# Tiles 6 and 7 joined on VectorE, and the last dense bank split by expert, in a one-core attention and mixture-of-experts kernel

## The reference

```
h = layernorm(x) * (1 + ca) + sa
x = x + ga * attention(h)            # 16 query heads, 4 key/value groups, causal
h = layernorm(x) * (1 + cb) + sb
logits = h @ gate_w.T                # 8 experts, the best two, softmax over the two
out = x + gb * sum over the two of  w_f * (expert_w[e_f] @ h + expert_b[e_f])
```

## Time and profile before

| | |
|---|---|
| median of 3 runs | 882.91 us (882.91 to 884.2) |
| profiled execution, its own time | 882.36 us |
| its span | 880.2 us |
| busy: TensorE, VectorE, ScalarE, GpSimd | 98%, 84%, 62%, 37% of the span |
| chain that ended last, by engine | TensorE 91%, VectorE 4%, ScalarE 1%, GpSimd 1%, DMA 1% |

### The profile page before, as it was taken

One profiled execution on the slowest core, in us unless ns is written; L12 is line 12 of the kernel. 1 busy time (PEld: TensorE's weight loads), 2 busy tenths in 40 slices (PEclk: granted clock), 3 DMA queues, 4 the chain that ended last, 5 costly groups with the idle time before them and its releaser, 6 DMA issues.

```text
span 880.2 us, 17025 instructions
## 1 busy us (share of the span) xinstructions
PE 863.9 (98%) x5433; PEld 772.0 (88%) x5433; DVE 741.2 (84%) x1686; ACT 541.9 (62%) x1249; POOL 325.9 (37%) x398
## 2 busy tenths in 40 slices
PE   8999999999999999999999999999999999999996
PEld 7888888888888888888888998999988888889995
DVE  6878888888888888878878888988888989888777
ACT  5686666666666666664666666666666666665462
POOL 3744122222222222140534444444422222577565
PEclk9999999999999999999999999999999999999999
DMA  7000800000000000300000000000000000442494
GB/s 270 1 12 14 287 13 13 13 12 12 12 12 12 12 12 13 108 7 7 0 26 13 14 13 13 13 13 14 13 13 13 9 6 13 150 151 89 140 285 128
DMA packets 37201, 43.34 MB, mean 49 GB/s; under 512 B 3104, under 2 KB 34366, under 8 KB 37054
## 3 DMA queue, kind: packets, MB, share of 16 engines
q1 hardware_dynamic: 34776, 36.20, 12.9%
q0 software_dynamic: 2304, 6.29, 2.3%
q10 hardware_dynamic: 56, 0.02, 0.0%
HBM read 32.28 MB, written 15.20 MB: 54 GB/s over the span
## 4 chain that ended last, share of the span: by engine, by line
PE 91%; DVE 4%; ACT 1%; issue 1%; POOL 1%; DMA 1%; POOLq 0%; SPq 0%; ACTq 0%
PE ps_t L1092 14%; PE ps_s L976 8%; PE ps_s L980 8%; PE ps_s L977 8%; PE ps_o L968 7%; PE ps_o L972 7%; PE ps_o L969 7%; PE ps_m L976 4%; PE ps_m L980 4%; PE ps_m L977 4%; PE ps_m L968 3%; PE ps_m L972 3%; PE ps_m L969 3%; PE ps_o L1102 1%; PE ps_t L976 1%
## 5 line engine op out<-in xcount | busy, mean ns | idle before, releaser
L1447 ACT ACTIVATE pt_hi<-ps_t 128x512 fp32r<-128x512 f32 (+2 forms) x320 | 170.8, 534 | 124.7 <-PE ps_t L1092 124.2
L1497 ACT ACTIVATE probs<-ps_s,neg_max 128x128 f32<-128x128 f32 (+7 forms) x256 | 189.8, 742 | 79.6 <-DVE neg_max L1893 76.7
L1902 DVE TENSOR_TENSOR pt_lo<-ps_t,pt_hi 128x512 fp32r<-128x512 f32 (+2 forms) x320 | 192.1, 601 | 13.0 <-ACT pt_hi L1447 9.0
L1893 DVE TENSOR_REDUCE neg_max<-ps_s 128x1 f32<-128x128 f32 (+7 forms) x256 | 192.3, 751 | 3.7
L724 POOL TENSOR_TENSOR q_lo<-raw,q_hi 128x512 fp32r<-128x512 f32 x60 | 77.4, 1289 | 310.6 <-ACT q_hi L1447 310.6
L1092 PE MATMUL ps_t<-ident,probs 128*128 128x128 f32 x1152 | 188.6, 272 | 0.9 <-DVE pt_lo L1902 0.9
L1092 PEld LDWEIGHTS ps_t<-ident,probs 128*128 128x128 f32 x1152 | 141.8, 141 | 20.5 <-DVE pt_lo L1902 4.9
L976 PE MATMUL ps_s<-k_hi,q_hi 128*128 128x512 f32 (+2 forms) x354 | 148.5, 419 | 2.4 <-ACT probs L1497 2.4
L1940 DVE SCALAR_TENSOR_TENSOR acc<-ps_m,rsum,acc 128x256 f32<-128x256 f32 x256 | 111.3, 476 | 16.3 <-PE ps_m L980 15.7
L980 PE MATMUL ps_s<-k_hi,q_lo 128*128 128x512 f32 (+2 forms) x354 | 123.4, 349 | 0.0
L1887 DVE TENSOR_TENSOR ps_s<-ps_s,mask 128x128 f32<-128x128 f32 x256 | 75.4, 295 | 56.7 <-PE ps_s L980 49.2
(11 more groups left out here) (341 smaller groups left out, 1717.5 us busy)
## 6 DMA issues: line engine op xcount, KB each, us to landing
slot_out_dram<-y_slot SPq DMA_DIRECT2D x38, 128.0 KB, 1.8
wq_raw<-in_L_attn_wq_dram SPq DMA_DIRECT2D x32, 128.0 KB, 2.3
wo_raw<-in_L_attn_wo_dram SPq DMA_DIRECT2D x32, 128.0 KB, 2.0
wkv_raw<-in_L_attn_wkv_dram SPq DMA_DIRECT2D x2, 1024.0 KB, 6.4
acc<-in_L_attn_x_dram SPq DMA_DIRECT2D x2, 1024.0 KB, 16.7
we_raw<-in_L_ffn_expert_w_dram SPq DMA_DIRECT2D x1, 2048.0 KB, 8.6
slot_rows<-slot_rows_dram SPq DMA_DIRECT2D x2, 1024.0 KB, 8.4
slot_rows_dram<-in_L_attn_x_dram SPq DMA_DIRECT2D x1, 1920.0 KB, 15.9
```

Of the source, the lines that this page charges most:

```text
L1447: return nc.scalar.activation(dst, src, ACT.Copy, scale=scale)
L1497: nc.scalar.activation(probs[par][:, prob_offset(i):prob_offset(i) + w], ps_s[:, i % 2, col:col + w], ACT.Exp, bias=neg_max[:, par, i:i + ...
L1893: nc.vector.tensor_reduce(neg_max[:, par, i:i + 1], ps_s[:, i % 2, col:col + w], AXIS_X, ALU.max, negate=True).then_inc(max_set, 1)
L1902: nc.vector.tensor_tensor(pt_lo[:, q % PT, lo:CH], ps_t[:, q % 2, lo:CH], pt_hi[:, q % PT, lo:CH].bitcast(F32), ALU.subtract).then_inc(pt_ ...
```

## The change

- GpSimd joins no tile; `weigh(j)` and `join_part` treat all tiles alike. Tiles 6 and 7 are weighted once on ScalarE and joined on VectorE, behind the last slot and before experts 6 and 7 of dense tile 1. SyncE stores them before dense tile 1.
- VectorE's join 8 goes into tile 2's mix, behind expert 5; join 9 behind tile 2's finish; joins 10 and 11 behind the last tile. ScalarE weights tile 9 before `mix_first(3)`.
- The last bank of dense tile 3 (experts 6 and 7) is made in two groups of 256 columns: expert 6 in the late bank, expert 7 in `ps_o`. `finish_last` adds both rows after expert 5 into `y_even`, then expert 6 and expert 7 to that sum, then gb and the residual.

```diff
@@ constants
-POOL_JOINS = (6, 7)
+SLOT_JOINS = 6
@@ SyncE
-            in_slots = joins_by(SLOTS1) // JOIN_OPS
-            for j in range(joins_by(SLOTS1 - 1) // JOIN_OPS, in_slots):
+            for j in range(joins_by(SLOTS1 - 1) // JOIN_OPS, NT):
                 store_joined(j)
             store_mixed(1)
-            for j in range(in_slots, NT):
-                store_joined(j)
+            store_joined(NT)
             store_mixed(2)
-            for j in range(NT, JOINS - 1):
+            for j in range(NT + 1, JOINS - 1):
                 store_joined(j)
             store_mixed(3)
             store_joined(JOINS - 1)
@@ GpSimd (pool_join is removed)
-            for lo, hi in ((0, NT), (NT, JOINS)):
-                for j in range(lo, hi):
-                    gather(j)
-                for j in POOL_JOINS:
-                    if lo <= j < hi:
-                        pool_join(j)
+            for j in range(JOINS):
+                gather(j)
@@ TensorE, experts(d, e2)
-                bank = late_bank(d, e2)
-                pair = slice(2 * e2, 2 * e2 + 2)
...
+                last_pair = 2 * e2 + 2 == EXPERTS and d + 1 == HALF
+                for lo in range(2 * e2, 2 * e2 + 2, 1 if last_pair else 2):
+                    these = slice(lo, lo + 1 if last_pair else lo + 2)
+                    bank = late_bank(d, e2)[:, 0:(these.stop - lo) * O] if lo % 2 == 0 else ps_o[:, 0:O]
+                    if lo % 2:
+                        pe.wait_ge(slot_out, ALL_SLOTS)
...
+                    last.then_inc(moe_mm, 1)
@@ ScalarE
                 if s + 2 == ALL_SLOTS:
-                    weigh(POOL_JOINS[0], 0)
-                    weigh(POOL_JOINS[0], 1)
-            weigh(POOL_JOINS[1], 0)
+                    weigh(SLOT_JOINS)
+            weigh(SLOT_JOINS + 1)
             slot_finish(ALL_SLOTS - 1)
-            weigh(POOL_JOINS[1], 1)
             hidden2_hi(3)
             mix_first(2)
             weigh(NT)
+            weigh(NT + 1)
             mix_first(3)
-            for j in range(NT + 1, JOINS):
-                weigh(j)
+            weigh(NT + 2)
+            weigh(NT + 3)
@@ VectorE
+            def finish_last():
+
+                d, par = HALF - 1, (HALF - 1) % 2
+                y = y_even[:, par, :]
+                dve.wait_ge(mixed, d * LATER_MIXES + LATER_MIXES - 2)
+                nc.vector.tensor_tensor(y, y, y_odd[:, par, :], ALU.add).then_inc(mixed, 1)
+                for e, bank in ((EXPERTS - 2, late_bank(d, EXPERTS // 2 - 1)), (EXPERTS - 1, ps_o)):
+                    dve.wait_ge(moe_mm, d * 4 + 4 + e % 2)
+                    dve.wait_ge(mixed, d * LATER_MIXES + e - 1)
+                    nc.vector.scalar_tensor_tensor(y, bank[:, 0:O], coef[:, d, e:e + 1], y,
+                                                   ALU.mult, ALU.add).then_inc(mixed, 1)
+                dve.wait_ge(mixed, d * LATER_MIXES + LATER_MIXES + 1)
+                nc.vector.tensor_tensor(y_sum[:, d, :], y, row_of["gb1"], ALU.mult).then_inc(ysum_set, 1)
+                dve.wait_ge(ysum_set, 2 * d + 1)
+                nc.vector.tensor_tensor(y_sum[:, d, :], y_sum[:, d, :], acc[:, NT + HALF + d, :],
+                                        ALU.add).then_inc(yout_set, 1)
...
+            for j in range(SLOT_JOINS, NT):
+                join(j)
             mix(1, {}, range(2 * DENSE_EARLY, EXPERTS))
             finish(1)
             hidden2_lo(3)
-            mix(2, {})
+            mix(2, {5: (NT,)})
             finish(2)
-            join(NT)
-            mix(3, {3: (NT + 1,), 5: (NT + 2,)})
-            finish(3)
-            if JOINS - 1 not in POOL_JOINS:
-                join(JOINS - 1)
+            join(NT + 1)
+            mix(3, {}, range(2, EXPERTS - 2))
+            finish_last()
+            join(NT + 2)
+            join(JOINS - 1)
```

More of the change, by code:

```diff
@@ L132, in joins_by @@
 def joins_by(i):
-    return max(0, min(JOIN_OPS * (NT - len(POOL_JOINS)), 4 * i // 3))
+    return max(0, min(JOIN_OPS * SLOT_JOINS, 4 * i // 3))
 def cuts_before(q):
@@ L475, in adaln_block @@
         join_step, joined_set, joined_done, weighed = sem("join_step"), sem("joined_set"), sem("joined_done"), sem("weighed")
-        pool_joined = sem("pool_joined")
-        vector_joins = [j for j in range(JOINS) if j not in POOL_JOINS]
-        weighs = [(j, f) for j in range(JOINS) for f in range(FREE if j in POOL_JOINS else 1)]
         bias_in, bias_step, bias_set = sem("bias_in"), sem("bias_step"), sem("bias_set")
@@ L588, in store_joined @@
             def store_joined(j):
[L590 to L593, removed]
+                sp.wait_ge(joined_set, j + 1)
                 sp.dma_start(out_tiles[:, j, :], picked[:, 0, j, :]).then_inc(joined_done, 16)
@@ L920, in gather @@
                         bass.IndirectOffsetOnAxis(ap=place[:, f, i:i + 1], axis=0)).then_inc(gathered[j % GATHERS], 16)
[L922 to L931, removed]
             inverse_deviation2(0)
@@ L1400, in experts @@
                     pe.wait_ge(*((first_mixed, 2 * d) if e2 == 0 else (mixed, (d - 1) * LATER_MIXES + 2 * e2)))
-                bank = late_bank(d, e2)
-                pair = slice(2 * e2, 2 * e2 + 2)
[L1403 to L1409, removed]
+                last_pair = 2 * e2 + 2 == EXPERTS and d + 1 == HALF
[4 more added lines that the diff above has]
+                        pe.wait_ge(slot_out, ALL_SLOTS)
+                    nc.tensor.matmul(bank, bias_ones[:, :], bias_planes[:, these, :].rearrange("p x o -> p (x o)"),
+                                     start=True, stop=False)
+                    for k in range(KE):
+                        w = [t[:, k, these, :].rearrange("p x o -> p (x o)") for t in (we_hi, we_lo)]
+                        last = held_late(bank, (h2_hi[d % 2][:, k, :], h2_lo[d % 2][:, k, :]), w, False, k == KE - 1,
+                                         (h2_lo_set, d + 1) if e2 == 0 and k == 0 else None)
+                    last.then_inc(moe_mm, 1)
             n = B * HEADS - 1
@@ L1665, in mix_first, with weigh @@
                                          scale=coef[:, d, e:e + 1]).then_inc(first_mixed, 1)
-            def weigh(j, f=0):
-                if f == 0:
-                    act.wait_ge(gathered[j % GATHERS], 32 * (j // GATHERS + 1))
-                w = (r_weight if j < NT else near["weight"])[:, f, j % NT:j % NT + 1]
-                nc.scalar.activation(picked[:, f, j, :], picked[:, f, j, :], ACT.Identity, scale=w).then_inc(weighed, 1)
+            def weigh(j):
+                act.wait_ge(gathered[j % GATHERS], 32 * (j // GATHERS + 1))
+                w = (r_weight if j < NT else near["weight"])[:, 0, j % NT:j % NT + 1]
+                nc.scalar.activation(picked[:, 0, j, :], picked[:, 0, j, :], ACT.Identity, scale=w).then_inc(weighed, 1)
             def weights_hi(u):
@@ L2361, in join_part @@
             def join_part(j, k):
-                first, second, o = picked[:, 0, j, :], picked[:, 1, j, :], 2 * vector_joins.index(j)
+                first, second, o = picked[:, 0, j, :], picked[:, 1, j, :], 2 * j
                 if k == 0:
                     w = (r_weight if j < NT else near["weight"])[:, 1, j % NT:j % NT + 1]
-                    dve.wait_ge(weighed, weighs.index((j, 0)) + 1)
+                    dve.wait_ge(weighed, j + 1)
                     nc.vector.scalar_tensor_tensor(first, second, w, first, ALU.mult, ALU.add).then_inc(join_step, 1)
```

## The result

| | before | changed |
|---|---|---|
| median of 22 runs | 882.95 us | 883.87 us |
| lowest | 882.7 us | 883.33 us |
| ratio changed / before | | 1.0012, 95% interval 1.0007 to 1.0018 |
| profiled execution, span | 882.36, 880.2 us | 883.83, 882.1 us |

The change costs 0.9 us, with an interval of 0.6 to 1.6. The prediction said 0.35 more than before, 883.3 within 882.3 to 884.4, and "within 0.2%" with a chance of 0.93. Time and class fit. Both kernels' times fall into two groups about 1.7 us apart (the slower one has 5 of 22 executions before, 7 of 22 changed), and inside either group the changed kernel is 0.8 to 0.9 us slower.

What follows compares the result with a forecast made beforehand. VectorE's list plus its holes was taken to bound the end. +0.27 us for that list and 0.08 for the final stores gave +0.35: execution 882.7, plus 0.55 to the median, 883.3 us; range 882.3 to 884.4.

Steps and rivals of the forecast that it cites:

- That the gathers are not freed by the joins alone: GpSimd's gather 8: the last slot's store holds it once the joins leave, so it starts only 1.08 us earlier.
- the third rival: VectorE at join 8: gather 8 starts no earlier and VectorE stands until 867.91, +1.34 us; chance 0.05.
- slower, at join 8: Join 8 waits while dense tile 2's banks lie ready: +1.34 us, or 2.1 with slow store issue; chance 0.05.
- Late gathers: All 0.70 us of issue follows the landing, or the store takes 3.2 us: end +0.7 to +1.1, 883.8; chance 0.25.
- The stall at join 8: VectorE waits about 1 us for tile 8's weighting, ready work queued behind; its list ends at 878.30, +0.27 us.
- The joins on VectorE cost nothing: Joins of tiles 6 and 7 fit VectorE's wait for TensorE's bank before 860.13: zero, 2.6 us without that cover.
- The doubled operations give 0.84 us back to no avail: Dense tile 1's two final VectorE operations drop from 0.84 to 0.42 us each; lost again before the next bank.
- The split bank: Last bank by expert: seven more TensorE matmuls go unseen; VectorE's finish gains one dependent step, 0.12 us.
- The final stores: SyncE issues three stores in 1.3 us against two at the end: 0 to 0.8 us, taken as 0.08.
- the second rival: Gathers only 0.3 to 0.7 us earlier, through late issue or landing: end +0.7 to +1.1, 883.8; chance 0.25.

Runs made afterwards that it cites:

- f4: Changed kernel with the joins of tiles 6 and 7 made over one column instead of 256; 1.0000 of the kernel before.
- e2: Changed kernel with the last bank whole and the old finish; 0.9999 of the kernel before.
- e3: Kernel before with only the last bank split and the last tile's new finish, GpSimd keeping its joins; 1.0006 of the kernel before.
- e1: Changed kernel with join 8 moved back behind the finish of dense tile 2; 1.0004 of the kernel before.
- f2: Changed kernel with join 8 back behind the finish of dense tile 2, repeated on another chip; 1.0004 of the kernel before.
- h3: Changed kernel with join 8 late, last bank whole, GpSimd's waits in store order, and join 10 behind expert 3 of the last tile; 0.9978 of the kernel before.
- h1: Kernel before, unchanged, run again on the third other chip for a trace of its tail; 909.7 us.
- g1: Changed kernel with join 8 late, last bank whole and GpSimd's waits in store order, on the third other chip; 0.9995 of the kernel before.
- h2: Changed kernel, unaltered, run again on the third other chip; 0.9999 of the kernel before.
- f1: Changed kernel, unaltered, run again on the second other chip; 0.9998 of the kernel before.

## Why the prediction was right where it was, and which term failed

*That the gathers are not freed by the joins alone: right in kind, wrong in size.* The prediction said that the store of the last slot takes over, and put gather 8 at 862.03, 1.08 us earlier, from a landing in 2.7 us and 0.29 us plus three steps. By the copy's clock that is +3.52; it came at +4.67, outside the 862.0 to 862.5 that the prediction had named as its sign. Two errors of about equal size make up the 1.15 us. The store landed in 3.23 us instead of 2.7, and the step from landing to gather was 1.02 us instead of 0.41. The nearest row that I took, the scatter behind VectorE's table, was the wrong one: the 0.70 us of issue in the chain was not overlap with the joins but a cost that follows the last wait. I had it as a bound and not as the value. Why the scatter started 0.29 us behind its releaser and a gather needs the whole 0.70 is open. The store's 3.23 us is the longest of the fourteen traces; yet 3.2 stood in the earlier trace rows, and the prediction's "nothing in the trace holds the last slot's store beyond 861.9" overlooked it. The 2.3 us that the prediction took from the Trainium skill ("DMA: Bandwidth & Descriptors", Anatomy of one DMA) is that section's fit for DMAs that GpSimd issues; this store is SyncE's, and none of the fourteen traces has less than 2.6.

What occurred in this trace is the third rival, "slower, at join 8", in its first form, and I had given it 0.05: gather 8 does not start earlier at all, it comes later than the rival's mark (862.7, which is +4.19), and VectorE ends 1.42 us later where the rival said 1.34. "Late gathers", with 0.25, had the right two conditions, but each alone.

*The stall at join 8: right in mechanism, sized from the failed term.* The prediction had join 8 starting at 866.83, +8.32; it started at +9.30. It stood idle for 2.05 us where I had said about 1. The 0.98 us later start runs undiminished through VectorE's list to the end, since nothing else waits there. With 0.16 us more in the finish, it accounts for 1.14 of the 1.15 us between the predicted end of VectorE, +19.79, and the measured +20.94. The additive reading of the list was sound: from join 8 to the last tile's sum it had 6.49 us, and 6.49 were measured.

*The joins on VectorE cost nothing: right*, and shown by f4. *The doubled operations give 0.84 us back to no avail: right*: 862.01 and 862.47 take 0.42, and the next bank hides it.

*The split bank: right that TensorE's part is not seen; the finish was under-priced.* Expert 6 was ready near 872.5 and wanted at 875.34. I had 0.12 us for the dependent chain, and it costs 0.28; the rest lies in the steps of 0.53 and 0.59 us ahead of the two additions, each with one more wait in VectorE's queue. By its time alone the split was not told apart (e2, e3).

*The final stores: 0.08 us assumed*; the last store took 2.1 us to the end, as before, so nothing.

*The sum.* +0.35 was forecast; +1.39 by the profile's tail, +0.92 by the medians. Other executions on the first chip with shorter landings than this one could explain the gap between those two, and the profiled execution before (882.36) was faster than all 22 timed ones; neither was followed up. That the time fell inside the range is in part luck: both mis-sized terms make the kernel slower, and the range reached so far only because it held the second rival and 0.55 us more for the spread of executions. That join 8's stall causes the measured 0.9 us on the first chip rests on the traces of that chip. The experiment that would have shown it by time ran only on chips on which a later wait can cover it, so it is not shown.

## What to carry to other kernels

Freeing an engine is worth only the distance to the next thing its consumer waits for: before counting the 5 us of work taken away, look up when the last input of the freed operation lands, and add the queue's waits and the issue that come after that landing. When work is moved ahead of operations that are ready, in a list that is otherwise full, its wait goes to the end undiminished, as on the first chip; where a later wait stands in the list, moving the work back may win nothing, as in e1 and f2. A hole that the list has is the place for it, and h3, which uses one, is the one version that was clearly faster. If a term has two rows that bound it and one of them is the same operation at the same place, take that one. Read the spread of a landing beside its one value.

## What the runs showed of the hardware that was not expected

The same program took 882.95 us on one chip and 907.5 to 909.7 on three others, with a granted clock of 0.996 and 0.985. On the third of these its median moved from 907.7 to 909.7 us between two measurements 10 minutes apart. Of the 27 us in h1, 22 arise between the first scatter (826.53) and the last slot's copy (883.99), where semaphores that TensorE raises are seen late by ScalarE and VectorE (9.2 us behind the recorded end of the matmul at 865.68) and where the granted clock falls to 0.50 after TensorE has stood idle.

In the tail the same signal, for experts 4 and 5 of the last tile, is late by 1.6 us (g1) to 3.2 us (h2) behind the recorded end of the last matmul, while TensorE's matmuls are recorded at their usual spacing of 0.23 us and the granted clock in that stretch is 1.00; in f1 it delays nothing. What delays the signals is not settled: nothing that was run touches them, and it is not excluded that the recorded starts of the matmuls are at fault instead. One coincidence may help whoever goes on. In h1 all the long waits of this kind lie in or just behind a run of GpSimd's indirect DMAs (826.5 to 836.5, 843.6 to 863.6 and 888.3 to 898.0), and between 870 and 888, where GpSimd issues none, there is none. But the first chip runs the same indirect DMAs without such waits. A verdict on half a microsecond from one kind of chip did not carry over to the other.
